# Four attention layers in one kernel: an order of its own for each engine in place of one shared order

## The chip, the cores and the metric

One core of one Trainium2 chip. The metric is device time in microseconds (us) of one execution, the median of several runs. PE is TensorE, DVE VectorE, ACT ScalarE, POOL GpSimd, SP SyncE, which only issues DMAs here.

## The reference, cut to what matters

Eight images of 16 x 16 positions and 128 channels, float32, go through four layers:

```python
# layer 0: group norm, then full attention over 256 tokens
h = group_norm(x, gamma, beta, groups=16)
attn = softmax((h @ wq + bq) @ (h @ wk + bk).T * C ** -0.5)
x = h + attn @ (h @ wv + bv)
# layer 1: attention inside each image row (16 keys), 16 channels for q and k
q, k = relu(x @ Wq + bq), relu(x @ Wk + bk)
x = gamma1 * softmax(q @ k.T, per row) @ (x @ Wv + bv) + x
# layer 2: full attention, 16 channels for q and k
x = gamma2 * softmax((x @ Wb) @ (x @ Wc).T) @ (x @ Wd) + x
# layer 3: 8 heads of 16; keys and values from a pooled image of 8 x 8
xp = avg_pool_3x3_stride2(x)
q, k, v = x @ w_q + b_q, xp @ w_k + b_k, xp @ w_v + b_v      # reshaped to heads row by row
x = softmax(q @ k.T / 4) @ v @ w_o + b_o + x
```

## The kernel before

Images are the unit of work: `g` is an image, and some steps take a pair. The feature map of an image lies in SBUF as `xT[g]`, channels by 256 tokens. Every step of a layer is one PE operation group into one PSUM bank, evacuated by ACT or DVE. Steps, in the names of the code: `norm` (ACT), `qk`, `v`, `scores` (PE), row maxima (DVE), the exponential with its sum (ACT), `scale` (POOL in layer 0, DVE in layer 2, line 594), `probT` (PE turns the probabilities, ACT copies them, line 470), `o` (values applied on PE, line 794; DVE adds the result to `xT`, line 610). In layer 1 `turn` takes the place of `scale` and `probT` (DVE, then POOL line 360).

Layer 3 for one image: `pool` on POOL (lines 383 to 392); `q`, `kv` and `x` on PE (line 805; 801 and 802, one bank for a pair; 864), ACT evacuates q, kT and x, DVE the values (line 680); `scores3` (PE line 819, two banks); DVE two maxima and two subtractions (618, 621); ACT two exponentials in place (488); `halves3` on POOL (368); sums and reciprocal on DVE (628, 631); `share3`, two scalings on POOL (375), for the last image on DVE (638); `probT3` (PE 832, two banks; ACT 492); `pv` (PE 846, ACT 499); `y` (PE 871; DVE 691 adds x); store on SP (312).

The keys of a pair go through DRAM: ACT writes kT, SP stores it (line 269), and eight DMAs (line 260) place it on the diagonal of `kdiag`, of which there are two, cleared at the start by DVE and POOL (line 253). For pair 0 SP issues four of the eight and ACT four. The values go the same way into `vdiag` (284, 291); SP's list of these (lines 293 to 308) is written out by hand.

What sets the order: lines 144 to 163 give every step a distance from the one before it in steps; image `g` is due `g` later than image 0. Sorted, this is one `sequence`. PE, DVE, ACT and POOL each walk the same sequence and do those steps of it that are theirs. PE's tiles take the eight PSUM banks in turn (`place[...] % BANKS`), and `begin` waits until the tile eight places earlier is drained. Each engine works in order: a wait holds everything behind it on that engine. From `kv` of pair 0 on, PE's order is: o 4, probT 6, x 0, q 1, o 5, probT 7, x 1, q 2, o 6, x 2, kv 2, q 3, o 7, x 3, q 4, scores3 0, x 4, kv 4, q 5, scores3 1, x 5, q 6, scores3 2, x 6, kv 6, q 7, scores3 3, x 7, probT3 0, scores3 4, pv 0, probT3 1, scores3 5, pv 1, probT3 2, scores3 6, y 0, pv 2, probT3 3, scores3 7, y 1, pv 3, probT3 4, y 2, and so on to y 7. On POOL all eight poolings stand before the first `halves3`.

Of the kernel before, what the change touches and what calls it, by code (L numbers as in the profile page):

```python
# [18 lines left out]
PAIR = 2  # L19
# [7 lines left out]
KEY_BUFFERS = 2  # L27
# [56 lines left out]
def build(nc, x, packs, out):  # L84
# [7 lines left out]
    with ctx:  # L92
# [3 lines left out]
        def sem(name):  # L96
# [47 lines left out]
        steps = [("norm", 0, 0), ("qk", 0, 4), ("v", 0, 2), ("scores", 0, 2), ("scale", 0, 2), ("probT", 0, 3), ("o", 0, 3)]  # L144
        steps += [("qk", 1, 1), ("v", 1, 1), ("scores", 1, 2), ("turn", 1, 2), ("o", 1, 2)]
        steps += [("qk", 2, 1), ("v", 2, 1), ("scores", 2, 3), ("scale", 2, 2), ("probT", 2, 2), ("o", 2, 2)]
        steps += [("pool", 3, 1), ("q", 3, 3), ("kv", 3, 0), ("x", 3, 1), ("scores3", 3, 4), ("share3", 3, 2), ("halves3", 3, -1), ("probT3", 3, 3),
                  ("pv", 3, 1), ("y", 3, 2)]
        due, start = [], 0
        for n, (kind, layer, distance) in enumerate(steps):  # L150
            start += distance
            for g in range(IMAGES):

                if kind != "kv" and (kind, layer) not in (("qk", 1), ("qk", 2)):
                    due.append((start + g, -n, kind, layer, g))
                elif g % 2:
                    due.append((start + g, -n, kind, layer, g - 1))
        sequence = [task[2:] for task in sorted(due)]
        sequence.insert(sequence.index(("qk", 1, 0)), ("setup", 1, 0))
        sequence.insert(sequence.index(("qk", 2, 0)), ("bias", 3, 0))  # L160
        sequence.insert(sequence.index(("qk", 0, 1)), ("group var", 0, HALF))
        sequence.remove(("kv", 3, 0))
        sequence.insert(sequence.index(("q", 3, 0)) + 1, ("kv", 3, 0))
# [5 lines left out]
        parts_of = {"scores3": ("scores0", "scores1"), "probT3": ("probT0", "probT1"),  # L169
                    "norm": (), "scale": (), "turn": (), "pool": (), "setup": (), "halves3": (), "share3": ()}  # L170
        for step, layer, g in sequence:
            if (step, layer) == ("scores", 2):
                order += [(step, layer, g), (step, layer, g + 1)] if g % 2 == 0 else []
            else:
                order += [(kind, layer, g) for kind in parts_of.get(step, (step,))]
# [813 lines left out]
```

## Time and profile before

| | |
|---|---|
| median of 3 runs | 131.18 us (129.76 to 133.01) |
| the profiled execution | 131.21 us, its span 129.4 us |
| busy us: PE, DVE, ACT, POOL | 111.2, 81.6, 76.6, 66.8 |
| mean granted clock of PE | 0.96 |
| chain that ended last | PE 60%, DVE 16%, ACT 13%, DMA 4%, POOL 3% |

The busy time of PE counts pipelined matmuls to their modelled ends. The start of one group less the start of the one before it, where PE did not wait, is what the group takes from PE. The same holds for DVE, ACT and POOL, where neighbours overlap by some 0.1 us. "Idle" with an arrow is the time that an engine stood still just before an instruction, and what released it.

### The profile page before, as it was taken

What the parts mean: (1) busy time and instruction counts of PE and PEld (TensorE: products, weight loads), DVE (VectorE), ACT (ScalarE), POOL (GpSimd) and SP (SyncE); (2) the same over time, 40 slices, a digit from 0 to 9 for tenths busy, and PEclk for the clock granted to TensorE, in tenths of its full rate; (3) what the DMA queues carried; (4) which work ended last, traced back from release to release, by engine and by line L of the source; (5) the groups of instructions that cost most, each with busy time, mean ns of one, the idle gap of its engine ahead of it and who ended that gap; (6) DMA issues with size and microseconds to landing.
All of it is one profiled execution on the core that took longest, in us unless ns stands there. A gap on an engine that the chain in (4) does not pass through costs nothing.

```text
span 129.4 us, 3874 instructions
## 1 busy us (share of the span) xinstructions
PE 111.2 (86%) x1516; PEld 86.3 (67%) x1516; DVE 81.6 (63%) x201; ACT 76.6 (59%) x228; POOL 66.8 (52%) x116
## 2 busy tenths in 40 slices
PE   6687999999999999999989999848943996949881
PEld 4465899987876878767668797526413675739780
DVE  4867767554324464588878823459699299888112
ACT  0445397698884756648796837165617637474450
POOL 8303629898801211321018988872977929963000
PEclk9999999999999999999999999998698599995999
DMA  3960000000000000000000027244565560120123
GB/s 74 331 211 0 0 5 3 0 3 3 0 5 0 5 0 0 5 0 0 0 0 0 5 72 133 77 100 123 107 91 122 105 62 5 46 79 2 51 75 88
DMA packets 15521, 6.43 MB, mean 50 GB/s; under 512 B 9360, under 2 KB 14864, under 8 KB 15504
## 3 DMA queue, kind: packets, MB, share of 16 engines
q1 hardware_dynamic: 13744, 4.66, 16.4%
q10 hardware_dynamic: 1760, 1.53, 4.5%
q8 instruction: 12, 0.20, 0.7%
q14 instruction: 5, 0.04, 0.1%
HBM read 4.61 MB, written 1.57 MB: 48 GB/s over the span
## 4 chain that ended last, share of the span: by engine, by line
PE 60%; DVE 16%; ACT 13%; DMA 4%; POOL 3%; issue 2%; ACTq 0%; DVEq 0%
PE bank L794 10%; PE bank L739 9%; DVE negmax L618 6%; PE bank L758 5%; ACT prob L488 5%; PE bank L832 5%; PE bank L846 4%; ACT probT L492 4%; DMA x_all<-in_x_dram 4%; PE bank L778 4%; PE bank L791 3%; DVE prob L621 3%; PE bank L730 3%; PE bank L819 3%; PE bank L723 2%; PE bank L768 2%
## 5 line engine op out<-in xcount | busy, mean ns | idle before, releaser
L432 ACT ACTIVATE prob<-bank,negmax 128x256 f32<-128x256 f32 (+1 forms) x48 | 19.3, 409 | 13.3 <-DVE negmax L583 10.4
L610 DVE SCALAR_TENSOR_TENSOR xT<-bank,packed,xT 128x256 f32<-128x256 f32 x24 | 11.6, 483 | 16.1 <-PE bank L794 12.1
L488 ACT ACTIVATE prob<-prob 128x512 f32<-128x512 f32 x16 | 9.8, 631 | 15.3 <-DVE prob L621 15.3
L794 PE MATMUL bank<-probT,v 128*128 128x256 f32 x64 | 16.9, 387 | 0.4 <-ACT probT L470 0.4
L739 PE MATMUL bank<-packed,xT 128*128 128x128 f32 (+1 forms) x96 | 15.6, 286 | 0.2 <-ACT prob L432 0.2
L375 POOL TENSOR_TENSOR prob<-prob,inv 128x512 f32<-128x512 f32 x14 | 14.4, 1051 | 0.5 <-DVE inv L631 0.5
L739 PEld LDWEIGHTS bank<-packed,xT 128*128 128x128 f32 x96 | 13.1, 191 | 1.9 <-issue 1.2
L360 POOL TENSOR_TENSOR probT<-turned,packed 128x256 f32<-128x256 f32 x8 | 4.9, 612 | 18.4 <-DVE turned L605 18.4
L368 POOL TENSOR_TENSOR probT<-prob 128x512 f32<-128x512 f32 x8 | 10.2, 1269 | 7.6 <-ACT prob L488 7.6
L846 PE MATMUL bank<-probT,vdiag 128*32 128x32 f32 x512 | 6.8, 206 | 7.9 <-ACT probT L492 7.8
L794 PEld LDWEIGHTS bank<-probT,v 128*128 128x128 f32 x64 | 11.2, 190 | 3.2 <-issue 1.6
L618 DVE TENSOR_REDUCE negmax<-bank 128x8 f32<-128x512 f32 x16 | 10.0, 668 | 4.9 <-PE bank L819 4.9
L819 PE MATMUL bank<-kdiag,qT 64*32 64x256 f32 x256 | 10.1, 430 | 3.0 <-DMA kdiag<-k_rows 2.3
L846 PEld LDWEIGHTS bank<-probT,vdiag 128*32 128x32 f32 x512 | 5.9, 117 | 9.9 <-issue 9.8
L470 ACT ACTIVATE probT<-bank 128x512 f32<-128x512 f32 x16 | 9.4, 601 | 3.6 <-issue 1.8
L832 PE MATMUL bank<-packed,prob 128*128 128x128 f32 x64 | 10.2, 311 | 0.0
L621 DVE TENSOR_TENSOR prob<-bank,negmax 128x512 f32<-128x512 f32 x16 | 10.2, 682 | 0.0
L778 PE MATMUL bank<-packed,prob 128*128 128x128 f32 x64 | 9.7, 273 | 0.0
L492 ACT ACTIVATE probT<-bank 128x512 f32<-128x512 f32 x16 | 8.8, 594 | 1.4 <-PE bank L832 1.4
L432 ACT ACTIVATION_READ_ACCUMULATOR prob<-bank,negmax 128x1 f32 x48 | 9.5, 199 | 0.0
L819 PEld LDWEIGHTS bank<-kdiag,qT 64*32 64x32 f32 x256 | 4.4, 118 | 7.0 <-issue 5.4
L413 ACT ACTIVATE v<-bank 128x256 f32<-128x256 f32 (+1 forms) x24 | 9.1, 383 | 0.0
(111 smaller groups left out, 237.4 us busy)
## 6 DMA issues: line engine op xcount, KB each, us to landing
kdiag<-k_rows SPq DMA_DIRECT2D x28, 64.0 KB, 2.2
out_dram<-x_all SPq DMA_DIRECT2D x8, 128.0 KB, 1.9
x_all<-in_x_dram SPq DMA_DIRECT2D x2, 256.0 KB, 4.2
x_all<-in_x_dram ACTq DMA_DIRECT2D x2, 256.0 KB, 5.5
vdiag<-v_rows SPq DMA_DIRECT2D x8, 64.0 KB, 3.3
packed<-in_pack_dram ACTq DMA_DIRECT2D x1, 321.0 KB, 5.8
k_rows<-kT SPq DMA_DIRECT2D x4, 64.0 KB, 1.9
kdiag<-k_rows ACTq DMA_DIRECT2D x4, 64.0 KB, 3.4
```

Source lines behind the costliest of these rows:

```text
L375: nc.gpsimd.tensor_tensor(p, p, inv[g][:, t, :].unsqueeze(2).broadcast_to([128, HEADS, KEYS]), ALU.mult)\
L432: last = nc.scalar.activation(prob[g][:, t, 0:keys], psum("scores", layer, g)[:, keys * t:keys * t + keys], ACT.Exp, bias=negmax[g][:, t, ...
L488: nc.scalar.activation(prob[g][:, t, :], prob[g][:, t, :], ACT.Exp).then_inc(s_exp3, 1)
L492: nc.scalar.activation(probT[g][:, t, :], psum(f"probT{t}", 3, g)[:, :], ACT.Copy)\
L618: nc.vector.tensor_reduce(out=negmax[g][:, h, :], in_=banks[h], op=ALU.max, axis=AX.X, negate=True).then_inc(s_max3, 1)
L621: nc.vector.tensor_tensor(view(prob[g][:, h, :], HEADS), banks[h], negmax[g][:, h, :].unsqueeze(2).broadcast_to([128, HEADS, KEYS]), ALU.add)\
L739: last = mm(ps[:, wide * t:wide * t + wide], xT[g][:, 128 * t:128 * t + 128], weights, start=True, stop=True)
L778: last = transpose(ps[:, TOK * k + 128 * t:TOK * k + 128 * t + 128], prob[g][:, t, 128 * k:128 * k + 128], ident)
L794: last = mm(ps[:, 0:TOK], vals[:, k, 0:C], probT[g][:, 0, TOK * k:TOK * k + TOK], start=k == 0, stop=k == TILES - 1)
L819: last = mm(banks[h][STRIP * s:STRIP * s + STRIP, wide * t:wide * t + wide].rearrange("p (c m k) -> p c k m", c=HCHUNKS, m=HKEY), qT[g][ro ...
L832: last = transpose(ps[:, 128 * p:128 * p + 128], prob[g][:, t, 128 * p:128 * p + 128], ident)
L846: last = mm(ps[STRIP * p:STRIP * p + STRIP, at:at + HTOK], vdiag[g // 2][:, HEADS * (g % 2) + j, :, :].rearrange("p c e -> p (c e)"), prob ...
```

## The change

The shared sequence goes. A table `slots` gives for each engine, step and layer the place of each image in that engine's list; each engine walks its own list (`turns`), SP too. The lists agree on what is done, not on the order. In PE's list first images run ahead: the last `o` of layer 2 (image 7) has place 115, behind `scores3` of images 0 and 1; the value products of layer 0 for images 0 and 1 stand ahead of the second group variance; DVE does both score blocks of images 0 and 1 in layer 3 before it updates image 7; POOL does `halves3` of image 0 before the pooling of image 7. On DVE the last image's scaling is a step of its own (`last3`).

`kv` becomes two tiles, `k` and `v`, each in a bank of its own and with its own place; the values' evacuation no longer waits for kT. There are three `kdiag` (KEY_BUFFERS), each cleared by one memset, two of them by POOL at the start. All eight placements of pair 0 are issued by SP. Some waits are added that the old order made needless (image ready for q, packed weights of layers 1 and 3).

```diff
-KEY_BUFFERS = 2
+KEY_BUFFERS = 3
...
+        slots = {
+            "tensor": {
+                ("v", 0): [0, 1, 7, 8, 13, 17, 22, 27],
+                ("group var", 0): [2],
+                ("qk", 0): [3, 4, 5, 10, 12, 15, 16, 19],
+                ("scores", 0): [6, 9, 11, 14, 20, 24, 25, 31],
+                ("probT", 0): [18, 23, 26, 29, 35, 37, 42, 48],
+                ("o", 0): [21, 30, 32, 34, 40, 43, 49, 54],
+                ("v", 1): [28, 36, 45, 47, 50, 57, 61, 70],
+                ("qk", 1): [33, 39, 52, 59],
+                ("scores", 1): [38, 41, 46, 51, 55, 56, 62, 68],
+                ("o", 1): [44, 53, 58, 63, 64, 66, 72, 77],
+                ("qk", 2): [60, 67, 73, 88],
+                ("bias", 3): [65],
+                ("scores", 2): [69, 74, 79, 94],
+                ("v", 2): [71, 76, 81, 84, 86, 96, 99, 104],
+                ("probT", 2): [75, 80, 82, 87, 89, 97, 102, 108],
+                ("o", 2): [78, 83, 85, 91, 98, 101, 106, 115],
+                ("k", 3): [90, 100, 109, 122],
+                ("v", 3): [92, 114, 120, 139],
+                ("q", 3): [93, 105, 113, 116, 117, 121, 124, 135],
+                ("x", 3): [95, 103, 110, 112, 119, 126, 129, 145],
+                ("scores3", 3): [107, 111, 118, 123, 127, 130, 134, 138],
+                ("probT3", 3): [125, 128, 132, 137, 142, 144, 150, 151],
+                ("pv", 3): [131, 136, 141, 143, 146, 149, 154, 155],
+                ("y", 3): [133, 140, 147, 148, 152, 153, 156, 157],
+            },
+            "scalar": {
+                ("norm", 0): [0, 1, 2, 5, 6, 7, 8, 9],
+                ("v", 0): [3, 4, 10, 12, 14, 16, 20, 26],
+                ("scores", 0): [11, 13, 15, 18, 21, 23, 25, 29],
+                ("probT", 0): [17, 19, 22, 27, 30, 32, 36, 40],
+                ("v", 1): [24, 34, 38, 39, 41, 45, 48, 54],
+                ("qk", 1): [28, 33, 42, 47],
+                ("scores", 1): [31, 35, 37, 43, 44, 46, 50, 51],
+                ("qk", 2): [49, 52, 56, 71],
+                ("scores", 2): [53, 55, 59, 60, 65, 66, 74, 77],
+                ("v", 2): [57, 61, 63, 67, 68, 75, 80, 82],
+                ("probT", 2): [58, 62, 64, 69, 73, 76, 81, 85],
+                ("k", 3): [70, 79, 86, 96],
+                ("q", 3): [72, 83, 89, 91, 94, 95, 98, 108],
+                ("x", 3): [78, 84, 88, 92, 93, 101, 105, 118],
+                ("scores3", 3): [87, 90, 97, 99, 103, 107, 111, 112],
+                ("probT3", 3): [100, 102, 106, 109, 113, 116, 120, 121],
+                ("pv", 3): [104, 110, 114, 115, 117, 119, 122, 123],
+            },
+            "vector": {
+                ("qk", 0): [0, 1, 3, 5, 10, 11, 15, 17],
+                ("scores", 0): [2, 4, 7, 9, 16, 19, 20, 25],
+                ("scale", 0): [6, 8, 12, 14, 21, 22, 24, 30],
+                ("setup", 1): [13],
+                ("o", 0): [18, 23, 26, 27, 32, 33, 39, 42],
+                ("scores", 1): [28, 31, 35, 38, 41, 43, 49, 54],
+                ("turn", 1): [29, 36, 37, 40, 45, 46, 51, 57],
+                ("o", 1): [34, 44, 47, 48, 50, 53, 59, 65],
+                ("bias", 3): [52],
+                ("scores", 2): [55, 56, 61, 62, 66, 67, 75, 76],
+                ("scale", 2): [58, 60, 63, 68, 71, 74, 77, 80],
+                ("o", 2): [64, 69, 70, 72, 78, 79, 81, 84],
+                ("v", 3): [73, 86, 88, 100],
+                ("scores3", 3): [82, 83, 87, 90, 92, 94, 97, 99],
+                ("share3", 3): [85, 89, 91, 93, 96, 98, 102, 103],
+                ("y", 3): [95, 101, 105, 106, 107, 108, 109, 110],
+                ("last3", 3): [104],
+            },
+            "gpsimd": {
+                ("scores", 0): [0, 1, 2, 4, 7, 9, 10, 13],
+                ("scale", 0): [3, 5, 6, 8, 11, 12, 14, 17],
+                ("late", 3): [15],
+                ("turn", 1): [16, 18, 19, 20, 21, 22, 23, 24],
+                ("pool", 3): [25, 26, 27, 28, 29, 30, 31, 33],
+                ("halves3", 3): [32, 34, 36, 38, 40, 42, 45, 46],
+                ("share3", 3): [35, 37, 39, 41, 43, 44, 47],
+            },
+            "sync": {
+                ("write keys", 3): [0, 2, 5, 7],
+                ("place keys", 3): [1, 4, 6, 10],
+                ("write values", 3): [3, 8, 11, 15],
+                ("place values", 3): [9, 12, 13, 16],
+                ("store", 3): [14, 17, 18, 19, 20, 21, 22, 23],
+            },
+        }
+        def turns_of(engine):
+            every = []
+            for (step, layer), row in slots[engine].items():
+                every += [(slot, step, layer, IMAGES // len(row) * n) for n, slot in enumerate(row)]
+            return [task[1:] for task in sorted(every)]
+        turns = {engine: turns_of(engine) for engine in slots}
...
-        QUARTERS, EARLY, LATE = 2, 1, 0
+        EARLY = 1
...
+            eng.memset(kdiag[n][:, :, :, :], 0.0).then_inc(s_zero, 1)
+        ZEROS = KEY_BUFFERS + IMAGES // PAIR
...
-                sp.wait_ge(s_key_rows, i + 1)
+                wait_drained(sp, "k", 3, PAIR * i)
                 sp.dma_start(k_dram[i].rearrange("e (m n) -> (e m) n", m=HEADS), kT[i][:, :]).then_inc(s_keys_out[i], 16)
 
             def place_keys(i):
 
                 if i == 0:
-                    sp.wait_ge(s_zero, QUARTERS + IMAGES // PAIR)
+                    sp.wait_ge(s_zero, ZEROS)
                 if i >= KEY_BUFFERS:
                     for t in range(TILES):
                         wait_filled(sp, f"scores{t}", 3, PAIR * (i - KEY_BUFFERS) + PAIR - 1)
                 sp.wait_ge(s_keys_out[i], 16)
-                for c in range(SHARED if i == 0 else HEADS):
+                for c in range(HEADS):
...
-                wait_drained(sp, "kv", 3, PAIR * i)
+                wait_drained(sp, "v", 3, PAIR * i)
...
+            for step, layer, g in turns["sync"]:
+                if step == "write keys":
+                    write_keys(g // PAIR)
+                if step == "place keys":
+                    place_keys(g // PAIR)
+                if step == "write values":
+                    write_values(g // PAIR)
+                if step == "place values":
+                    place_values(g // PAIR)
+                if step == "store":
...
+                if step == "late":
+                    clear_values()
...
-                wait_filled(act, "kv", 3, g)
-                nc.scalar.activation(kT[g // PAIR][:, :], psum("kv", 3, g)[:, 0:PAIR * PTOK], ACT.Identity, bias=part["bk3"])\
-                    .then_inc(s_key_rows, 1)
+                wait_filled(act, "k", 3, g)
+                nc.scalar.activation(kT[g // PAIR][:, :], psum("k", 3, g)[:, 0:PAIR * PTOK], ACT.Identity, bias=part["bk3"])\
+                    .then_inc(*drained_by("k", 3, g))
...
-                    if g == 1:
-                        act.wait_ge(s_zero, QUARTERS + IMAGES // PAIR)
-                        act.wait_ge(s_keys_out[0], 16)
-                        for c in range(SHARED, HEADS):
-                            place_chunk(act, 0, c)
...
+                if step == "v":
...
-                    dve.wait_ge(s_key_rows, g // PAIR + 1)
...
+                    wait_filled(dve, "v", 3, g)
+                    nc.vector.tensor_tensor(vt[g // PAIR][:, :], psum("v", 3, g)[:, 0:C], part["bv3"], ALU.add).then_inc(*drained_by("v", 3, g))
...
+                if step == "last3":
+                    share_last(IMAGES - 1)
...
-            def keys_values3(g):
+            def pooled(g):
 
                 pe.wait_ge(s_pool, (g + 2) * POOL_STEPS)
-                ps, pooled = begin("kv", 3, g), poolT[g // PAIR][:, :, :, :].rearrange("p i h w -> p (i h w)")
-                mm(ps[:, 0:PAIR * PTOK], part["w3k"], pooled, start=True, stop=True)
-                mm(ps[:, PAIR * PTOK:PAIR * PTOK + C], pooled, part["w3v"], start=True, stop=True).then_inc(*filled_by("kv", 3, g))
+                if g == 0:
+                    pe.wait_ge(s_packed[W3], 16)
+                return poolT[g // PAIR][:, :, :, :].rearrange("p i h w -> p (i h w)")
+            def keys3(g):
+                rows = pooled(g)
+                mm(begin("k", 3, g)[:, 0:PAIR * PTOK], part["w3k"], rows, start=True, stop=True).then_inc(*filled_by("k", 3, g))
+            def values3(g):
+                rows = pooled(g)
+                mm(begin("v", 3, g)[:, 0:C], rows, part["w3v"], start=True, stop=True).then_inc(*filled_by("v", 3, g))
 
             def queries3(g):
+                image_ready(3, g)
+                if g == 0:
+                    pe.wait_ge(s_packed[W3], 16)
```

## Rows read from the trace of the kernel before

**Rows 1.** Windows: stretch, length, busy us (instructions) PE PEld DVE ACT POOL, clock, DMA share, GB/s

```profile
13.20:80.04 66.84, 65.76 (x564) 53.05 (x565) 40.21 (x115) 47.41 (x166) 33.31 (x74) 1.00 0.05 11
80.04:129.40 49.36, 35.82 (x891) 26.41 (x889) 32.26 (x61) 24.33 (x51) 28.61 (x36) 0.90 0.35 76
```

**Rows 2.** Waits, the span: who waited for whom, us, times, longest

```profile
ACT prob L488 <- DVE prob L621: 15.3, 8, 3.2
PE bank L846 <- ACT probT L492: 7.8, 5, 3.9
```

**Rows 3.** Timeline of PE round 79 us: start, us, line, form, instructions

```profile
78.08 0.38 PE L864 MATMUL bank<-packed,xT 128*128 128x128 f32 x2
78.74 0.60 PE L805 MATMUL bank<-xT,packed 128*128 128x256 f32 x2
79.18 1.03 PE L794 MATMUL bank<-probT,v 128*128 128x256 f32 x4
80.04 0.38 PE L864 MATMUL bank<-packed,xT 128*128 128x128 f32 x2
```

**Rows 4.** Timeline of PE in the steady part of layer 3, and one slow turn

```profile
109.93 1.09 PE L819 MATMUL bank<-kdiag,qT 64*32 64x256 f32 x32
110.96 0.71 PE L871 MATMUL bank<-packed,qT 128*128 128x128 f32 x4
111.60 0.76 PE L846 MATMUL bank<-probT,vdiag 128*32 128x32 f32 x64
112.32 1.07 PE L832 MATMUL bank<-packed,prob 128*128 128x128 f32 x8
116.34 1.70 PE L832 MATMUL bank<-packed,prob 128*128 128x128 f32 x8
```

**Rows 5.** Timeline of DVE: layer 3's sums, maxima, subtractions; the last scaling

```profile
106.01 0.68 DVE L628 TENSOR_REDUCE inv<-probT 128x16 f32<-128x512 f32 x1
106.89 1.22 DVE L618 TENSOR_REDUCE negmax<-bank 128x8 f32<-128x512 f32 x2
108.03 1.28 DVE L621 TENSOR_TENSOR prob<-bank,negmax 128x512 f32<-128x512 f32 x2
116.65 2.11 DVE L638 TENSOR_TENSOR prob<-prob,inv 128x512 f32<-128x512 f32 x2
```

**Rows 6.** Windows of POOL alone (poolings; layer 3), and one halves operation of its timeline

```profile
67.20:85.50 18.30, 15.59 (x40) 1.00 0.26 54
85.50:117.70 32.20, 24.05 (x22) 0.88 0.42 83
...
110.05 1.28 POOL L368 TENSOR_TENSOR probT<-prob 128x512 f32<-128x512 f32 x1
```

**Rows 7.** Chain that ended last, its end: start, us, what

```profile
123.52 1.09 ACT probT L492 x2
124.75 0.75 PE bank L846 x48
126.72 0.42 DVE x_all L691
```

**Rows 8.** Timeline of SP, keys of pair 1, and of PE, the block that waits

```profile
79.66 0.34 SPq L269 DMA_DIRECT2D k_rows<-kT  x1
81.58 4.60 SPq L260 DMA_DIRECT2D kdiag<-k_rows  x8
...
88.00 1.10 PE L819 MATMUL bank<-kdiag,qT 64*32 64x256 f32 x32 [2.35 <-DMA kdiag<-k_rows]
```

**Rows 9.** Groups by form: POOL's clearing; timeline: POOL's first power

```profile
L253 POOL MEMSET kdiag<- 128x4096 f32 x1 | 3.5, 3512 | 0.1
...
9.81 1.03 POOL L325 TENSOR_TENSOR var_gn<-var_gn,neg_half 128x4 f32<-128x4 f32 x1 [5.41 <-DVE var_gn L534]
```

**Rows 10.** Timeline of DVE: one scaling of layer 2 beside pooling, another

```profile
67.25 0.92 DVE L594 TENSOR_TENSOR prob<-prob,inv 128x512 f32<-128x512 f32 x1
73.03 0.69 DVE L594 TENSOR_TENSOR prob<-prob,inv 128x512 f32<-128x512 f32 x1
```

More of the change, by code:

```diff
@@ L149, in build @@
[L149 to L159, printed above, removed]
@@ L168, in build @@
         order += [("group mean", 0, HALF)]
-        parts_of = {"scores3": ("scores0", "scores1"), "probT3": ("probT0", "probT1"),
-                    "norm": (), "scale": (), "turn": (), "pool": (), "setup": (), "halves3": (), "share3": ()}
-        for step, layer, g in sequence:
+        parts_of = {"scores3": ("scores0", "scores1"), "probT3": ("probT0", "probT1")}
+        for step, layer, g in turns["tensor"]:
             if (step, layer) == ("scores", 2):
-                order += [(step, layer, g), (step, layer, g + 1)] if g % 2 == 0 else []
+                order += [(step, layer, g), (step, layer, g + 1)]
+            elif step == "group var":
+                order.append((step, layer, HALF))
             else:
@@ L229, in width_of, with nth @@
             return C + 1 if layer == 0 else C
-        def nth(step, layer, g):
-            return [(s, l, n) for s, l, n in sequence if s == step].index((step, layer, g)) + 1
+        def nth(step, layers, layer, g):
+            return [(l, n) for s, l, n in turns["vector"] if s == step and l in layers].index((layer, g)) + 1
         def strip_of(g, n):
@@ L330, in _, with clear_values @@
                 nc.gpsimd.tensor_scalar(part[w], part[w], part[gate], None, ALU.mult).then_inc(s_gated, 1)
-            def clear_late():
-                for late in range(QUARTERS - LATE, QUARTERS):
-                    clear_kdiag(nc.gpsimd, late)
+            def clear_values():
                 for i in range(IMAGES // 2):
                     nc.gpsimd.memset(vdiag[i][:, :, :, :], 0.0).then_inc(s_zero, 1)
-            for step, layer, g in sequence:
-                if step == "scores" and layer == 0:
+            for step, layer, g in turns["gpsimd"]:
+                if step == "scores":
                     pool.wait_ge(s_raw, g + 1)
@@ L457, in _ @@
             nc.scalar.activation(part["w0r"], fuse[:, C + 2:C + 3], ACT.Copy, scale=float(C) ** -0.5).then_inc(s_fused, 1)
-            for step, layer, g in sequence:
+            for step, layer, g in turns["scalar"]:
                 if step == "norm":
                     normalise(g)
-                if step == "qk" and layer > 0:
+                if step == "qk":
                     queries_keys(layer, g)
@@ L657, in _ @@
             factors(HALF)
-            for step, layer, g in sequence:
-                if step == "qk" and layer == 0 and g >= EARLY_QUERIES:
+            for step, layer, g in turns["vector"]:
+                if step == "qk" and g >= EARLY_QUERIES:
                     queries_keys0(g)
@@ L921, in _ @@
             group_means(HALF)
-            for step, layer, g in sequence:
+            for step, layer, g in turns["tensor"]:
                 if step == "qk":
+                    if layer == 1 and g == 0:
+                        pe.wait_ge(s_packed[W12], 16)
                     project(layer, g)
                 if step == "group var":
-                    group_variances(g)
-                if step == "v":
+                    group_variances(HALF)
+                if step == "v" and layer == 3:
+                    values3(g)
+                elif step == "v":
                     if layer == 1 and g == 0:
@@ L936, in _ @@
                         score(layer, g)
[L937 removed]
+                    else:
                         score_pair(g)
```

62 lines of the change are left out of this document (12 added, 50 removed).

## The prediction

> **What bounds the kernel now.** I read first the busy time of each engine in two stretches, cut where PE finishes the last attention output of the third layer (o2 of image 7) [rows 1]. Up to 80.04 us PE is busy 65.76 of 66.84 us at a granted clock of 1.00: PE bounds the first three layers, and a consumer counts there only if it makes PE wait. Behind 80.04 no engine is full: PE 35.82, DVE 32.26, POOL 28.61 and ACT 24.33 of 49.36 us, clock 0.90. There the engines wait for one another. The table of waits says how [rows 2]: ACT's exponentials of the last layer wait 15.3 us for DVE's subtraction, and PE's value products wait 7.8 us for ACT's copies of the turned probabilities, which stand in ACT's order behind such an exponential. So the gain can come only from the second stretch, 38% of the span, by more overlap in it and with what lies before it. The profiled execution took 131.21 us, 1.81 more than its span of 129.4, and lies on the median shown (131.18), so no correction is made between them.
>
> **Up to o2 of image 7 (call its end E).** PE's work in layers 0 to 2 is the same; only pieces of layer 3 trade sides. By differences of starts [rows 3] x, k and v cost 0.22 each (0.66 for an x and a joined kv), q 0.44, o 0.86; a score block costs 1.03 [rows 4]. Before E the old order has four q, two kv and three x: 1.76 + 0.88 + 0.66 = 3.30. The new one has three q, three k, two v, four x and two score blocks: 1.32 + 1.98 + 2.06 = 5.36. E = 80.04 + 2.06, less the old idle time of 1.08, plus the new one. For that I take 1.1 for the ordinary waits and 0.5 for the first keys (below): E = 82.6, 2.6 us **later** than now. I followed image 0 and 1 through the new table as far as the joined qk of layer 1, with each consumer's own queue ahead of it, and found no wait on PE; behind it the consumers have about as many PE steps of distance as now.
>
> **Behind E, DVE.** The timetable puts two score blocks of layer 3 on DVE ahead of the update of image 7. A block costs two maxima at 1.14 together and two subtractions at 1.28, about 2.4; sums and reciprocal 0.88 [rows 5]. The first block leaves PE 3.7 before E (a turn of layer 2, taken at 0.44 like q, k, x, x and v 0.9, a block 1.03, q 0.44, o 0.86), so DVE is free for the update at E - 3.6 + 4.8 = E + 1.2 and done at E + 1.7. This is the edit's cost: POOL's last pooling and then everything of image 7 stand behind it. DVE then has six blocks (14.4), eight sums (7.0), three value evacuations (0.75), the last scaling 2.1 [rows 5] and eight y at 0.4 (3.3): 27.6, so DVE alone cannot end before E + 29.
>
> **Behind E, POOL.** Eight poolings are 15.59 busy, 1.95 each, 2.06 with gaps; eight halves and seven scalings are 24.05, with halves at 1.28 from one start to the next 1.25, so (24.05 - 8 x 1.25)/7 = 2.0 for a scaling [rows 6]. Pooling 7 runs E + 1.7 to 3.8; then seven halves (8.75) and seven scalings (14.0) follow: E + 26.5 for the last scaling, if none waits. I laid DVE's and ACT's orders beside this. Sums of image 1 end at E + 6.4, of 2 at 9.7, 3 at 13.0, 4 at 16.7, 5 at 20.0, of 6 at 24.2; POOL wants them at 8.3, 11.5, 14.7, 17.9, 19.9, 24.4. The exponentials of image 7 end at 23.1 and POOL wants them at 23.2. So POOL runs nearly full where now it is busy 24.05 of 32.20, 75% [rows 6]; DVE is nearly full beside it.
>
> **Behind E, PE and the end.** PE still has five q, four x, one k, two v, six blocks, and eight each of turned probabilities (1.07), values (0.72) and y (0.5): 2.2 + 1.5 + 6.2 + 8.6 + 5.8 + 4.0 = 28.3 [rows 4], and waits some 3. After the last scaling (POOL E + 26.5, DVE's for image 7 E + 27.5) come the second half of a turn 0.5, ACT's two copies 1.09, the value products 0.75, a copy and a wait 0.5, y 0.5, the addition 0.42 [rows 7]: E + 31.7. The store and the end take 129.4 - 127.14 = 2.26 [rows 7]. So E + 34.0 against 80.04 + 49.36 now. To this I add two slips. The last pair's values leave DVE at E + 22.6 and stand on SP behind the first store, which has gone at 16; written and placed they land between E + 28 and 29.4, where their products want them at 28.9: 0.5. And the clock: a turn of both halves took 1.70 in a slow stretch against 1.07 [rows 4], after PE had been waiting; one such in the closing chain costs 0.6, two 1.2: I take 1.0, with 0 and 3 as bounds (five pairs at most stand between the middle and the end).
>
> **The sum.** 82.6 + 34.0 + 0.5 + 1.0 = 118.1 of span, and 1.81: **119.9 us**.
>
> **The other edits.** Keys: the write of a pair starts when kT is made, the eight placements start 1.92 later and took 4.60 to issue, and PE's block got them at 88.00, 8.3 after kT's write began [rows 8]. In the new order PE has 8.5 us of work between k of pair 0 and its first scores; kT adds 0.5, so the wait is about 0.5, and what stands behind it is the last o2: counted in E. ACT no longer issues half of pair 0; it gains about 2 us of issue time, off the path, and SP loses them, on this chain: that is in the 8.3, which is a case with all eight on SP. In the Trainium skill, "DMA: Bandwidth & Descriptors" (Issuing engines are not separate DMA queues) says that several issuers save only the issue time; by it this edit costs 2 us at most, the chain above has it already. The third diagonal adds one clearing of 3.51 on POOL; POOL idles 5.41 there ahead of its first power [rows 9], so it is hidden; without that cover the first normalised image would come up to 3.5 later. Its use: the placement of pair 2 need not wait for the scores of image 1, nor that of pair 3 for those of image 3. On SP these placements come at about E + 1.6 and E + 8, and the scores leave PE at E - 1.5 and E + 5.2, so I give it nothing, with a bound of 1 us gained. Separate k and v tiles cost a bank more and no PE time (0.22 twice); they free DVE from waiting for kT.
>
> **Rivals.** (1) SP's queue sets the pace. SP's list from the first kT (E - 13.2) to the last keys is four writes, four placements and two pairs of values. With 4.0 per placement, pair 3's keys land at E + 14.2 where PE wants them at 14.4; at 4.60 each [rows 8] they are 2.4 later, and behind the values' placings another 0.5: **122.5**. For it: no slack in my table; against: DVE wants the block 1 us after PE. Chance 0.16. (2) The in-order wait of ACT's copies behind exponentials stays: in the new order the copies for image 4 stand behind two exponentials. If half of the 7.8 [rows 2] comes back: **123.8**. Chance 0.12. (3) DVE and POOL block each other. DVE's scaling in layer 2 took 0.92 beside the pooling and 0.69 free of it [rows 10], and now all eight stand beside poolings. If each of eight is 0.23 longer and on the path: 1.8, **121.7**; but POOL waits for o2 there. Chance 0.04. The Trainium skill, "SBUF — State Buffer" (Who interferes with whom), has the rule: a DVE operation with two SBUF inputs and a POOL operation that reads SBUF take turns at one port. By that rule this overlap would be worth nothing; the row shows a third longer, and I go by the row. (4) Slower: 116 PE steps go up to E in an order in which a bank, of eight, must be drained before PE goes on. If the consumers come late by 0.1 us a step, as they would when one lags behind its place, E moves by 11.6 and nothing is won (**131.5**); from 0.12 on it is slower by over 2%, and at 0.15 it is **137**. For it: one engine's delay passes to all through fixed orders. Against: idle time of 1.08 in the old order [rows 1], and my partial trace of the new one. Chance 0.06 for no change, 0.05 for slower. That the change does nothing, because PE was full anyway, is excluded by PE's 13.5 idle us behind 80.04.
>
> **How the numbers follow.** My forecast has 0.57 (115.8 to 122; the low end is without the slips of 1.5, the 0.5 at the keys and the idle time of 1.1, and 1.0 gained by the diagonal). Faster by over 2%, which is what can be told from no change here, is the forecast and rivals 1 to 3: 0.57 + 0.16 + 0.12 + 0.04 = 0.89; within 2% 0.06; slower 0.05. The range of 8 in 10 goes from 115.8 to 125.8: its top is rival 2 with the clock's bound of 3 in place of 1.0 (123.8 + 2.0), and it leaves out (4), 0.11, and some of each side.
>
> **What would show it.** E (the end of o2 of image 7 on PE) between 81.5 and 84; the stretch behind it 34 to 37 long; POOL busy over 85% from pooling 7 to its last scaling; DVE without waits over 1 us between the third block and the last scaling; PE's blocks waiting under 1 us for keys; the granted clock behind E at 0.9 or more. An E past 88 makes the prediction wrong by rival 4; PE waiting for kdiag in several blocks by rival 1; ACT's copies late by rival 2.

## The result: 118.56 us, a ratio of 0.899, and the profile after

The changed kernel took 118.56 us (median of 4 runs, 116.9 to 120.31), the kernel before 131.65 beside it (129.76 to 133.01): ratio 0.8989, interval 0.8918 to 0.9059. Forecast were 119.9 us, within 115.8 to 125.8. The profiled execution took 116.9 us, 1.9 more than its span; it is the fastest of the four, and PE's clock was granted in full in it (the others' mean clocks are 0.998, 0.986 and 0.985). Some executions of either kernel are a per cent or two slower, most of them at a lower clock: the ratios here and below leave them out, while medians and ranges take all.

The page of the changed kernel: span, busy time by engine, and the share of each engine in the chain that ended last.

```profile
span 115.0 us, 3883 instructions
PE 107.4 (93%) x1516; PEld 83.3 (72%) x1516; DVE 80.2 (70%) x201; ACT 76.8 (67%) x228; POOL 70.9 (62%) x117
PE 73%; POOL 11%; DVE 7%; DMA 4%; issue 1%; ACT 1%; ACTq 0%; DVEq 0%
```

Windows of the changed kernel, cut at the end of o2 of image 7 (columns as in [rows 1]; the first starts with the span, and the next at the second group variance, as in [rows 1]):

```profile
0.00:80.76 80.76, 77.40 (x693) 61.33 (x693) 52.09 (x146) 53.91 (x179) 45.91 (x91) 1.00 0.16 42
14.59:80.76 66.17, 66.16 (x625) 53.01 (x625) 42.99 (x121) 48.16 (x165) 37.60 (x83) 1.00 0.08 22
80.76:115.00 34.24, 29.97 (x825) 22.02 (x823) 28.07 (x56) 22.89 (x49) 25.01 (x27) 1.00 0.43 88
```

The same windows of the kernel before, from the start of its span:

```profile
0.00:80.04 80.04, 75.34 (x626) 59.93 (x627) 49.30 (x140) 52.28 (x177) 38.17 (x81) 1.00 0.13 34
```

The end of o2 has moved by 0.72 only, and up to it PE now does 2.06 more work, the price of the two score blocks that run ahead (the smaller pieces that trade sides cancel). The stretch behind it fell from 49.36 to 34.24. PE's idle time there fell from 13.54 (49.36 less 35.82) to 4.27, which is 9.27; its busy time by 5.85, of which 2.06 are the moved blocks and the rest, 3.79, goes with the clock (0.90 before, 1.00 now).

Waits over the span of the changed kernel (who waited for whom: us, times, longest). The first answers to 15.3 in [rows 2]; PE's 7.8 us for ACT's copies ahead of the value products are no longer listed.

```profile
ACT prob L545 <- DVE prob L678: 3.6, 4, 1.4
PEld bank L901 <- POOL prob L434: 2.8, 5, 0.8
PE bank L762 <- ACT xT L466: 1.0, 1, 1.0
```

PE's timeline of the changed kernel (start, length, line, form, instructions, wait before it in brackets): the second group variance, the first score block of layer 3, o2 of image 7 and what follows. No block names a wait for keys; [rows 8] had 2.35.

```profile
14.59 0.36 PE L762 MATMUL bank<-spread,packed 128*128 128x8 f32 x2 [1.02 <-ACT xT L466]
75.63 1.09 PE L888 MATMUL bank<-kdiag,qT 64*32 64x256 f32 x32
79.89 1.03 PE L849 MATMUL bank<-probT,v 128*128 128x256 f32 x4
80.76 1.03 PE L874 MATMUL bank<-xT,packed 128*128 128x256 f32 x4
```

DVE's timeline of the changed kernel: the maxima of the first block, the update of image 7, and from there to the end every instruction with a wait, and the last scaling.

```profile
76.82 1.29 DVE L675 TENSOR_REDUCE negmax<-bank 128x8 f32<-128x512 f32 x2 [0.59 <-PE bank L888]
81.61 0.48 DVE L667 SCALAR_TENSOR_TENSOR xT<-bank,packed,xT 128x256 f32<-128x256 f32 x1
103.73 0.69 DVE L685 TENSOR_REDUCE inv<-probT 128x16 f32<-128x512 f32 x1 [1.05 <-POOL probT L427]
104.97 0.69 DVE L685 TENSOR_REDUCE inv<-probT 128x16 f32<-128x512 f32 x1 [0.27 <-POOL probT L427]
105.98 2.11 DVE L695 TENSOR_TENSOR prob<-prob,inv 128x512 f32<-128x512 f32 x2
109.28 0.87 DVE L746 TENSOR_TENSOR x_all<-bank,x_all 128x256 f32<-128x256 f32 x2 [0.53 <-PE bank L940]
111.78 0.97 DVE L746 TENSOR_TENSOR x_all<-bank,x_all 128x256 f32<-128x256 f32 x2 [1.62 <-PE bank L940]
```

POOL's timeline of the changed kernel: the start of pooling 7, the next half and the last scaling; between 82.17 and 106.94 no wait is listed.

```profile
82.17 0.40 POOL L442 TENSOR_TENSOR prob<-xT 128x128 f32<-128x128 f32 x1 [0.86 <-DVE xT L667]
84.23 1.28 POOL L427 TENSOR_TENSOR probT<-prob 128x512 f32<-128x512 f32 x1
104.89 2.05 POOL L434 TENSOR_TENSOR prob<-prob,inv 128x512 f32<-128x512 f32 x2
```

So from 82 to 105 DVE and POOL both run almost without a pause. The gain is best read on DVE, which does all of layer 3's maxima, subtractions, sums and the last scaling. The timeline of DVE in the kernel before has the first block here, and its last scaling at 116.65 [rows 5]:

```profile
82.66 1.29 DVE L618 TENSOR_REDUCE negmax<-bank 128x8 f32<-128x512 f32 x2 [1.93 <-PE bank L819]
```

| us, worked out from these | before | after | gain |
|---|---|---|---|
| DVE's first block starts | 82.66 | 76.82 | 5.84 |
| from there to its last scaling | 33.99 | 29.16 | 4.83 |
| (listed waits of DVE in it) | 6.14 | 1.32 | |
| from there to the end of the span | 12.75 | 9.02 | 3.73 |
| span | 129.4 | 115.0 | 14.4 |

The first line holds the running ahead (4.01 of it, by the run with the blocks put back below), the second the waits between engines. The third is the closing chain. The clock in it was 0.87 before and is 1.00 now, but that hardly shortened it: with the old order in the new code it took 12.22 at a clock of 1.00 (below).

### The profile page after: what moved, and what is told of

Its sections match the earlier page's. It is cut to its first block, busy times and chain, and to the rows that moved or that the text cites. A ratio compares the mean times of both kernels' runs of the same rounds, so it can differ in the third digit from the quotient of the medians.

```text
span 115.0 us, 3883 instructions
## 1 busy us (share of the span) xinstructions
PE 107.4 (93%) x1516; PEld 83.3 (72%) x1516; DVE 80.2 (70%) x201; ACT 76.8 (67%) x228; POOL 70.9 (62%) x117
## 4 chain that ended last, share of the span: by engine, by line
PE 73%; POOL 11%; DVE 7%; DMA 4%; issue 1%; ACT 1%; ACTq 0%; DVEq 0%
PE bank L849 12%; PE bank L794 10%; PE bank L833 6%; PE bank L813 6%; POOL prob L434 5%; PE bank L901 5%; DMA x_all<-in_x_dram 4%; PE bank L915 4%; PE bank L785 4%; PE bank L823 4%; PE bank L940 4%; PE bank L846 4%; POOL probT L427 3%; PE bank L778 3%; PE bank L888 3%; DVE negmax L675 2%
## 5 line engine op out<-in xcount | busy, mean ns | idle before, releaser
L794 PE MATMUL bank<-packed,xT 128*128 128x128 f32 (+1 forms) x96 | 14.5, 281 | 0.0
L419 POOL TENSOR_TENSOR probT<-turned,packed 128x256 f32<-128x256 f32 x8 | 5.5, 683 | 14.2 <-DVE turned L662 14.2
L640 DVE TENSOR_REDUCE negmax<-bank 128x2 f32<-128x64 f32 (+1 forms) x16 | 6.9, 451 | 3.7 <-PE bank L810 2.8
L901 PEld LDWEIGHTS bank<-packed,prob 128*128 128x128 f32 x64 | 6.8, 141 | 3.4 <-POOL prob L434 2.8
L888 PE MATMUL bank<-kdiag,qT 64*32 64x256 f32 x256 | 8.8, 382 | 0.1
L833 PEld LDWEIGHTS bank<-packed,prob 128*128 128x128 f32 x64 | 7.2, 141 | 1.9 <-issue 1.5
```

What stands on the lines that cost most here:

```text
L794: last = mm(ps[:, wide * t:wide * t + wide], xT[g][:, 128 * t:128 * t + 128], weights, start=True, stop=True)
L833: last = transpose(ps[:, TOK * k + 128 * t:TOK * k + 128 * t + 128], prob[g][:, t, 128 * k:128 * k + 128], ident)
L888: last = mm(banks[h][STRIP * s:STRIP * s + STRIP, wide * t:wide * t + wide].rearrange("p (c m k) -> p c k m", c=HCHUNKS, m=HKEY), qT[g][ro ...
L901: last = transpose(ps[:, 128 * p:128 * p + 128], prob[g][:, t, 128 * p:128 * p + 128], ident)
```

## Experiments

Each ratio is against the kernel before on the same chip.

### The changed kernel again

No edit.

> The changed kernel unaltered, as the reference for the three beside it on the same chip. Both theories: 117 to 119.5, ratio to the kernel before 0.89 to 0.91.

118.75 us (116.68 to 121.05), ratio 0.8945 (0.8873 to 0.9017). The next three ran on the same chip.

### Two diagonals

```diff
-KEY_BUFFERS = 3
+KEY_BUFFERS = 2
```

> The changed kernel with two key diagonals in place of three. Mine (the third buys nothing, its placements never come before the scores that free the buffer): the same within 0.5 us, blocks still without waits for keys. Rival (it is the third diagonal that lets the keys come in time): pair 2's placement, which started at 82.03, and pair 3's slip behind the scores, PE waits for keys at 88 and 95, 1 to 3 us slower.

118.48 us, ratio 0.8957 (0.8859 to 0.9054). The third diagonal is worth nothing that can be told, as the prediction had it (the changed kernel took 118.75 on this chip).

### The norm of image 3 first

```diff
-                ("norm", 0): [0, 1, 2, 5, 6, 7, 8, 9],   # ACT
+                ("norm", 0): [0, 1, 2, 2.5, 6, 7, 8, 9],
```

> The changed kernel with image 3's normalisation ahead of the first two value evacuations on ACT. In the changed kernel PE waits until 14.59 for the second group variance, whose bank is freed by that normalisation (ACT, ends 14.45). If PE sets the time all the way (no idle time on it from 14.59 to 80.76), the gain at the head, about 0.9 us, shows whole at the end: 0.7 to 1.0 us faster. Rival (POOL and DVE set the end): they start from PE's work too, so some 0.5 to 1.0; if instead the group variance then waits for something else (DVE's spread ends 13.40), under 0.3.

117.55 us (115.81 to 118.48), ratio 0.891 (0.8809 to 0.9011). The wait of 1.02 ahead of PE's second group variance is gone from its trace. The lowest run is 0.87 below the lowest of the unedited kernel; the intervals overlap. The wait's cause is thereby found: the group variance takes the PSUM bank that the norm of image 3 has still to read, and on ACT that norm stands behind two copies of v.

### The two first blocks behind o2 of image 7

```diff
-                ("scores3", 3): [107, 111, 118, ...   # PE
+                ("scores3", 3): [115.3, 115.6, 118, ...
-                ("scores3", 3): [87, 90, 97, ...      # ACT
+                ("scores3", 3): [92.3, 92.6, 97, ...
-                ("scores3", 3): [82, 83, 87, ...      # DVE
+                ("scores3", 3): [84.3, 84.6, 87, ...
-                ("pool", 3): [25, 26, 27, 28, 29, 30, 31, 33],   # POOL
+                ("pool", 3): [25, 26, 27, 28, 29, 30, 31, 31.5],
```

One q of ACT's list also moves behind them.

> The changed kernel with the first two score blocks of layer 3 behind the third layer's last output on PE, DVE and ACT, and POOL's last pooling ahead of its first halves; nothing else moved. Mine (the overlap of layer 3's first blocks with layer 2 is what fills PE): DVE starts its blocks about 3 us later, turns and values come later by it, PE idles behind the last output, 2 to 3.5 us slower. Rival (running ahead is worth nothing, the inner orders of layer 3 make the gain): within 1 us, since the last pooling comes 2.5 us earlier.

124.91 us (124.14 to 126.83), ratio 0.9548 (0.9473 to 0.9624): 6 us slower than the changed kernel, more than expected. Its PE timeline shows that the edit had made a wait of its own: a block wants a bank that the values of pair 1 hold, and on DVE these stand behind both moved blocks.

```profile
87.06 1.96 PE L888 MATMUL bank<-kdiag,qT 64*32 64x256 f32 x32 [4.33 <-DVE vt L736]
```

Hence the next, with DVE's evacuation of those values ahead of the first block:

```diff
-                ("v", 3): [73, 86, 88, 100],      # DVE
+                ("v", 3): [73, 83.5, 88, 100],
```

> As the run with the first two blocks behind the last output of layer 2 (ratio 0.955, 6 us slower than the changed kernel), but with DVE evacuating the values of pair 1 ahead of its first block. In that run PE stood 4.33 us until 87.06 for a bank that this evacuation had to free, since the move had shifted the rotation of the eight banks. If the loss was this bank: about 3.5 us come back, 120.5 to 122.5, and running ahead is worth the 2 to 3.5 us expected then. Rival (the blocks' lateness costs it all): still 124 to 126.

122.92 us (121.29 to 123.94), ratio 0.9362 (0.9264 to 0.9461). Its profiled execution, at a clock of 1.00 like that of the changed kernel, has a span of 119.5, 4.5 longer. DVE's first block and last scaling in it:

```profile
80.83 1.29 DVE L675 TENSOR_REDUCE negmax<-bank 128x8 f32<-128x512 f32 x2 [0.59 <-PE bank L888]
108.80 2.11 DVE L695 TENSOR_TENSOR prob<-prob,inv 128x512 f32<-128x512 f32 x2
```

DVE starts 4.01 later and the end is 4.5 later. The median is 1.99 below that of the run before (2.4 by the ratios), less than the 3.5 expected: some 2 of the 6 us were the bank. Running two blocks ahead is thus worth some 4 us of the 14.4. This is rather an upper bound: PE still waits 0.97 and 1.20 for DVE and ACT at 85.25 and 87.51 in this run, and whether the blocks' lateness or the shifted banks bring these waits was not tried.

### The old order in the new code

The table is replaced by the old steps, distances and sort, and SP's list by the old one; tiles, diagonals, issuers and waits stay as changed.

```diff
-        turns = {engine: turns_of(engine) for engine in slots}
+        sequence = [task[2:] for task in sorted(due)]
...
+        turns = {engine: [] for engine in ("tensor", "scalar", "vector", "gpsimd", "sync")}
+        for step, layer, g in sequence:
...
```

> The changed kernel's code with the old shared sequence on PE, ACT, DVE and POOL and SP's old list: key and value tiles apart, three diagonals, all placements by SP. Mine (the order is the whole gain, the other edits nothing): as the kernel before within 1.5 us, 130 to 133, E at 80 and a stretch behind it of 48 to 51. Rival (tiles apart and the third diagonal bring a good part): 124 to 128, since PE's wait of 2.35 for keys and DVE's waits of 4.0 for kT go.

129.59 us (127.91 to 130.99), ratio 0.9836 (0.9787 to 0.9885). The order is nearly all of the gain; the other edits are worth 1 to 2 us (1.2 by the medians, 2.1 by the ratio), which is more than the nothing that I gave them. DVE's first block and last scaling:

```profile
82.64 1.29 DVE L629 TENSOR_REDUCE negmax<-bank 128x8 f32<-128x512 f32 x2 [1.91 <-PE bank L842]
115.68 2.11 DVE L649 TENSOR_TENSOR prob<-prob,inv 128x512 f32<-128x512 f32 x2
```

Between them lie 33.04 us, 0.95 less than before; behind the last scaling 12.22, at a clock of 1.00. The kernel before listed this wait of its value evacuations, and this one none (waits over the span of the kernel before):

```profile
DVE vt L680 <- ACT kT L438: 4.0, 4, 1.3
```

So separate k and v tiles took DVE's waits for kT away. Its listed waits between the two lines above fell only from 6.14 to 5.21, since those for score blocks grew, and PE's wait for keys is still there with 2.20 (2.35 before).

### ACT in PE's order

ACT alone takes its steps in the order in which PE does them; the other engines keep their lists.

```diff
+        for key in slots["scalar"]:
+            if key not in (("norm", 0), ("scores", 2)):
+                slots["scalar"][key] = [slot + 10 for slot in slots["tensor"][key]]
...
```

> The changed kernel with ACT doing its evacuations and exponentials in the order in which PE makes the tiles, as one shared sequence would have it; PE, DVE, POOL and SP keep their lists. Mine (a consumer's own order is needed, because an exponential waits for DVE and holds up ACT's copies behind it): ACT's exponentials stand ahead of copies that are ready, PE waits for banks, 3 to 8 us slower. Rival (PE's new order alone makes the gain): under 1 us slower.

129.13 us (127.86 to 132.13), ratio 0.9791 (0.973 to 0.9853). More than expected: without its own list for ACT the new order keeps only some 2 of its 13 us. (The parts that these runs take out, 10 here, 4 for running ahead, 1 to 2 for the other edits, add up to more than the whole: they depend on one another.) Two waits over its span; the windows of PE and the others up to the end of its o2 of image 7; and DVE's first block and last scaling:

```profile
ACT prob L550 <- DVE prob L683: 13.0, 7, 3.4
ACT prob L499 <- DVE negmax L645: 7.9, 9, 2.7
```

```profile
14.59:88.00 73.41, 66.81 (x624) 52.71 (x624) 44.09 (x122) 48.22 (x165) 37.85 (x83) 1.00 0.07 19
```

```profile
83.10 1.29 DVE L680 TENSOR_REDUCE negmax<-bank 128x8 f32<-128x512 f32 x2 [0.59 <-PE bank L893]
116.05 2.11 DVE L700 TENSOR_TENSOR prob<-prob,inv 128x512 f32<-128x512 f32 x2
```

The old wait of 15.3 [rows 2] is back at 13.0. Read as in the table above, it costs 6.28 ahead of layer 3's first block, 3.79 between that and the last scaling, and 1.03 behind. So it is not layer 3 alone: up to 88.00 PE stands for 6.60 of 73.41 us, 0.01 in the changed kernel. That it waits there for evacuations behind exponentials, which wait 7.9 us for maxima (5.9 in the changed kernel), is my reading of the two rows.

### Half the work for POOL, for PE, for both

```diff
+                        p = p[:, 0:HEADS // 2, :]     # share3 on POOL
...
-                for p in range(PAIRS):                # probT3 on PE
+                for p in range(PAIRS // 2):
```

First POOL's edit alone, then PE's alone, then both with the last pair's values earlier on PE, DVE and SP. These kernels leave the other half of the scaling, or of the turning, out; they serve only to take work off an engine.

> The changed kernel with POOL scaling only the first half of the columns in layer 3 (seven scalings at 1.0 in place of 2.0), the other half left unscaled. If POOL's chain of halves and scalings sets the end, as my prediction had it: 4 to 6 us faster. If PE does, which was busy 18.25 of the last 18.3 us: 0.3 to 1.6 faster, its idle time between 80.76 and 94 being 1.5.

> The changed kernel with PE turning only half of layer 3's probabilities (two of four transposes in each bank, 0.5 us less for an image, 4 in all; the rest of the bank is left as it was). If PE sets the end: 2.5 to 4 us faster, until POOL's last scaling at 106.9 and what stands behind it (5 us) take over. If POOL's chain does: 0.3 to 1.0 faster, the turns behind the last scaling alone.

> POOL scales half of the columns and PE turns half of them in layer 3 (the other halves are left as they were), and the last pair's values are made, evacuated and written ahead. Each of the two halvings alone brought nothing (ratios 0.902 and 0.911 against 0.895 to 0.899). Mine now (the chains of PE, POOL and of the last values through DVE and SP end within a us of each other, so that only all together give time): 2 to 3.5 us faster than the changed kernel, ratio 0.865 to 0.885, DVE full then. Rival (DVE alone sets the end already, 27.64 of 31.54 us busy): within 1 us, ratio 0.89 to 0.91.

119.0 us, ratio 0.9016 (0.8946 to 0.9086); 119.09 us, 0.9106 (0.9052 to 0.9161); 119.06 us, 0.9104 (0.903 to 0.9177). None gains. That POOL alone sets the pace is refuted by the first, that PE alone does by the second. The third speaks against my idea that they do in turn, but less cleanly, because its edit made a wait of its own: a block of PE stands for a bank that DVE's evacuation of the values holds, as in the run with the blocks put back.

```profile
88.98 1.10 PE L889 MATMUL bank<-kdiag,qT 64*32 64x256 f32 x32 [1.82 <-DVE vt L737]
```

The stretch of DVE shows more than the total. Its first block and last scaling, in the order of the three:

```profile
79.26 1.29 DVE L676 TENSOR_REDUCE negmax<-bank 128x8 f32<-128x512 f32 x2 [0.59 <-PE bank L889]
108.32 1.29 DVE L696 TENSOR_TENSOR prob<-prob,inv 128x512 f32<-128x512 f32 x2
```

```profile
78.09 1.29 DVE L675 TENSOR_REDUCE negmax<-bank 128x8 f32<-128x512 f32 x2 [0.59 <-PE bank L888]
107.24 2.11 DVE L695 TENSOR_TENSOR prob<-prob,inv 128x512 f32<-128x512 f32 x2
```

```profile
76.54 1.29 DVE L676 TENSOR_REDUCE negmax<-bank 128x8 f32<-128x512 f32 x2 [0.60 <-PE bank L889]
106.11 1.29 DVE L696 TENSOR_TENSOR prob<-prob,inv 128x512 f32<-128x512 f32 x2
```

Between them lie 29.06, 29.15 and 29.57 us, where the changed kernel has 29.16, with listed waits of DVE of 1.10, 1.34 and 1.54 (1.32 there). The windows from 76 to 106, of the changed kernel and of the third run, show which engine stayed full (columns as in [rows 1]): PE and POOL have room in the second, DVE has not.

```profile
76.00:106.00 30.00, 28.45 (x710) 19.83 (x694) 27.77 (x56) 22.17 (x48) 27.54 (x36) 1.00 0.41 84
76.00:106.00 30.00, 24.13 (x574) 16.29 (x554) 27.64 (x54) 21.14 (x45) 22.19 (x35) 0.98 0.44 92
```

Behind the start of the last scaling the three take 9.78, 9.76 and 10.99, where the changed kernel has 9.02, so what the halves saved there (last section) was lost in the closing chain; why was not followed, but in the third run the clock there is 0.90. Whoever is relieved waits for DVE instead: POOL, halved, waits for the exponentials behind DVE's subtractions (its timeline in the first of the three).

```profile
92.49 1.26 POOL L427 TENSOR_TENSOR probT<-prob 128x512 f32<-128x512 f32 x1 [1.01 <-ACT prob L546]
99.64 1.28 POOL L427 TENSOR_TENSOR probT<-prob 128x512 f32<-128x512 f32 x1 [1.50 <-ACT prob L546]
```

### The update of image 7 between the first two blocks

```diff
-                ("o", 2): [64, 69, 70, 72, 78, 79, 81, 84],     # DVE
+                ("o", 2): [64, 69, 70, 72, 78, 79, 81, 82.5],
```

> The changed kernel with DVE's update of image 7 between the first two score blocks of layer 3 instead of behind both. If the late pooling of image 7 paces what follows, as the prediction said: pooling 7 starts 0.9 us earlier, 0.5 to 0.9 faster. If DVE's own work paces it: DVE waits 1.5 us for the output (80.8), its second block and all behind it come 1.5 to 2 later, 1 to 2 us slower. If PE does: 0 to 0.5 slower.

122.4 us (120.69 to 123.3), ratio 0.9284 (0.9172 to 0.9396): some 4 us slower, more than any of the three cases gave it. Pooling 7 does start 0.93 earlier, as its timelines of DVE and of POOL show, and nothing comes of it:

```profile
80.68 0.48 DVE L667 SCALAR_TENSOR_TENSOR xT<-bank,packed,xT 128x256 f32<-128x256 f32 x1 [1.66 <-PE bank L849]
107.90 2.11 DVE L695 TENSOR_TENSOR prob<-prob,inv 128x512 f32<-128x512 f32 x2
```

```profile
81.24 0.40 POOL L442 TENSOR_TENSOR prob<-xT 128x128 f32<-128x128 f32 x1 [0.21 <-DVE xT L667]
84.30 1.26 POOL L427 TENSOR_TENSOR probT<-prob 128x512 f32<-128x512 f32 x1 [0.96 <-ACT prob L545]
88.89 1.27 POOL L427 TENSOR_TENSOR probT<-prob 128x512 f32<-128x512 f32 x1 [1.32 <-ACT prob L545]
```

DVE stands 1.66 us for o2, and from its first block (76.54) to its last scaling it takes 31.36, 2.20 more. POOL, given its image earlier, stands and waits for exponentials. The rest of the 4 us lies behind the last scaling, 11.00 against 9.02, at a clock of 0.98 there. The delay is not DVE's alone: PE waits 2.20 at 83.70 for the bank that DVE's second block holds, and the clock from 80 to 92 is 0.86, so this run doesn't separate DVE's pace from PE's.

### Five more warming matmuls, with the norm first

```diff
             fuse_weights()
-            keep_warm(AFTER[3] // 2)
+            keep_warm(AFTER[3] // 2 + 5)
```

> Image 3's normalisation ahead, as in the run that came out at a ratio of 0.891, and five more dummy matmuls (0.11 us each) in PE's wait of 0.69 ahead of the second group mean. In some runs of the new order the granted clock fell to half between 12 and 19 us, which cost 2 to 4 us, and PE was busy 1.8 to 2.6 of 3 us there. If this idle time causes it: clock 0.995 or more in all runs, 115.5 to 117, ratio 0.88 to 0.89. Rival (the clock falls whatever stands there): as without the dummies, 117 to 118.5, or 0.1 slower.

116.97 us (115.85 to 117.71), ratio 0.8907 (0.8802 to 0.9012): the lowest median and the narrowest spread of all, 1.6 below the changed kernel's 118.56, though on another chip and with overlapping intervals. (PE's wait of 0.69 stands ahead of the second group mean; the variance follows it.) The ratio is that of the norm first alone (0.891), so no time of the five matmuls' own can be told; whether they steady the clock is discussed in the last section. I would take this version.

## Why the prediction was right, and where its steps were off

**The size and its place: right.** The stretch behind the third layer became 15.12 shorter, and 0.72 were given back ahead of it, PE's waits there fell to a third, and the clock there was 1.00 in the profiled execution (0.90 before), where 0.9 or more was forecast. The old order in the new code shows that the order brought it, the run with ACT in PE's order that a list of its own for ACT is the larger part (DVE's and POOL's lists were not tried so), and the blocks put back that running ahead is some 4 us.

**E: 82.6 forecast, 80.76 measured.** It lies below the 81.5 to 84 that was to show the prediction right. The moved work was right to the digit: PE's busy time up to E rose from 75.34 to 77.40, by 2.06. Its idle time did not rise by 0.5 but fell by 1.34 (4.70 to 3.36). The failed terms are the 1.1 of ordinary waits and the 0.5 for keys: from 14.59 on PE stands for 0.01 us in 66.17. What I had not seen is the wait of 1.02 ahead of that, at the second group variance; my trace of the table looked at work and queues, not at the turn of the banks.

**Behind E: 35.5 forecast, 34.24 measured.** Step by step, from E: the update of image 7 done at +1.33 (forecast 1.7), POOL's last scaling done at +26.18 (26.5), DVE's at +27.33 (27.5), the last addition at +31.99 (31.7), the end 2.25 later (2.26). So laying out the lists worked to within 0.4 at each step. One of these fits is partly a slip of adding: the terms that the prediction lists behind E + 27.5 come to E + 31.3 and not to the 31.7 that it went on with, so the closing chain, 4.66 from DVE's scaling to the last addition, was priced 0.9 too short in its terms. The two slips, 1.5, did not come: no product waited for values, and the clock stayed up in this execution. E and the stretch behind it make 1.84 and 1.26, the 3.1 between the forecast span of 118.1 and 115.0. The median of 118.56 lies closer to 119.9 than the profiled execution's 116.9, which is partly luck: two of the four executions had a mean clock of 0.986 and 0.985, and the prediction had no fall of the clock before E. The other signs that were named held (POOL is busy 24.46 of 24.77 us from pooling 7 to its last scaling), but for one wait of DVE of 1.05 where none over 1 was to be.

**POOL sets the end: wrong as a cause.** I wrote that everything of image 7 stands behind the late pooling, that POOL's chain sets the end and DVE is nearly full beside it. POOL is full, as said, and the chain that ended last passes through it; yet half its scalings buy nothing, and an earlier pooling 7, paid for with waits of DVE and PE, buys none either. In the runs of halves DVE's list still takes its 29 us and is full within 1.5 us of it, while PE and POOL have room. So DVE's list sets the pace from its first block to its last scaling, as far as relieving POOL and PE can show it. No run relieved ACT (22.17 of those 30.00 us busy) or took work off DVE itself, so what that would gain is open; the prediction's own sum had DVE at E + 29 beside it.

**The other edits.** Third diagonal nothing: right. k and v apart: no PE time, right; but that DVE no longer waits for kT was named and given no price, and with the old order the edits together are worth 1 to 2 us. How much of that remains under the new order was not tried.

**The rivals.** (1) SP's queue: no block waited for keys; the eight placements of a pair took 3.54 to 4.99 to issue, the range I feared, but were issued early. (Its own terms, 2.4 less the slack of 0.2, and 0.5, give 122.6, not 122.5.) (2) In-order copies on ACT: absent in the changed kernel, and real when brought back, at 10 us, not the 3.9 that I gave it, since it also holds up the layers before. (3) and (4): no sign of either up to E, where PE stands for 0.01 us from 14.59 on.

## What to carry to other kernels

Where engines work through fixed lists, a consumer can need an order of its own: an evacuation that PE waits for must not stand behind an operation whose input comes late from a third engine. Lay the lists beside each other by measured durations, and follow the turn of the PSUM banks too, since it ties steps together that share no data. A chain of work that passes through a full engine does not show that this engine sets the pace: relieve it, and see whether the time moves.

## What the runs showed of the hardware

**The clock can fall at the start of the work.** Windows of the second run of the changed kernel, and of the one with five more warming matmuls (columns as in [rows 1]):

```profile
12.00:15.00 3.00, 2.08 (x10) 1.78 (x10) 0.73 (x5) 2.27 (x6) 0.00 (x0) 0.57 0.00 0
15.00:18.00 3.00, 2.90 (x8) 2.48 (x9) 1.17 (x4) 0.00 (x0) 2.05 (x3) 0.50 0.00 0
```

```profile
12.00:15.00 3.00, 2.77 (x18) 2.33 (x18) 1.65 (x8) 1.74 (x5) 1.02 (x2) 1.00 0.00 0
15.00:18.00 3.00, 3.00 (x19) 2.76 (x19) 1.96 (x7) 2.27 (x6) 1.88 (x5) 1.00 0.02 5
```

From 15 to 18 the first has the lower level, 1.2 GHz; DVE's first block then starts at 79.34 instead of 76.82. The same kernel was granted 1.00 there in its first trace. What brings the fall is open. PE had stood for 0.69 us ahead of the second group mean, at 12.00; a mean of 0.57 from 12 to 15 means some 2.6 of 3 us at the lower level, so the fall began near 12.4, before the wait of 1.02:

```profile
15.10 0.57 PE L762 MATMUL bank<-spread,packed 128*128 128x8 f32 x2 [1.02 <-ACT xT L466]
```

Of the ten traces that have both waits four show an early fall, in two of them behind the wait of 1.02; the trace of the norm first, without that wait, shows it too (0.64 from 12 to 15). The kernel before has the same wait of 0.69, then one of 0.40, and its clock was 1.00. With the warming matmuls the wait of 0.69 is gone, and the mean clock of the four runs was 0.996 to 1.00; with the norm first alone it was 0.998 to 1.00 in five runs of six and 0.985 in one. So it is possible, not shown, that the matmuls prevent the fall.

**DVE's last scaling is held up by POOL's.** The two instructions take 2.11 us where POOL's last scaling runs beside them for 0.96 (105.98 to 106.94 in the changed kernel), and 1.29 in both runs where POOL's was halved and over within 0.10 of DVE's start. So 0.82 of 0.96 is lost, and it was so before [rows 5]. What it costs at the end is not shown, since neither of the two runs came out faster. The prediction went by a row with a third lost [rows 10]; by this pair, taking turns is nearer. The Trainium skill, "SBUF — State Buffer" (Who interferes with whom), says that a DVE operation with two SBUF inputs contends with a POOL operation that reads SBUF; these rows agree.
